# Stage ends and norms handled by token tile in a twelve-block transformer on one core

## The reference

```
x = x + cross_attention(layernorm(x), context of 4096 tokens, masks)   # 16 heads of 16
x = x + mixing(layernorm(x))
x = x + feed_forward(layernorm(x))
```

## Time and profile before

| | us |
|---|---|
| median of 3 runs | 1506.76 |
| the three runs | 1506.76, 1503.57, 1507.40 |
| span of the profiled execution (first to last instruction) | 1502.7 |
| time of the profiled execution, apart from its span | not given |
| median less span | 4.06 |
| busy: PE, DVE, ACT, POOL | 1371.0, 1010.4, 857.6, 567.3 |
| mean granted clock of TensorE, as a share of 2.4 GHz | 0.965 |

### The profile page before, as it was taken

How to read it: one execution, slowest core, us unless ns; L and a number is a source line. 1 busy time by engine, 2 the same in 40 slices (tenths; PEclk the granted TensorE clock), 3 DMA queues, 4 the chain that set the end, 5 groups by cost and what they waited for, 6 DMA issues and landing times. The chain is left out here.

```text
span 1502.7 us, 28955 instructions
## 1 busy us (share of the span) xinstructions
PE 1371.0 (91%) x10502; PEld 810.9 (54%) x10576; DVE 1010.4 (67%) x2314; ACT 857.6 (57%) x1308; POOL 567.3 (38%) x686
## 2 busy tenths in 40 slices
PE   8999797999999888699999888699999896999987
PEld 3766655455555456255555555255555582555555
DVE  4445486999999724778787053588884236888832
ACT  5143141899999621288888551167777211777762
POOL 4564252689989800655555340111110001111100
PEclk9999999799999978799999999899999998999999
DMA  8878998255456062266655195247776801667800
GB/s 265 280 255 256 245 258 274 33 77 83 65 82 146 2 89 39 53 96 90 88 81 143 59 185 202 75 71 109 104 113 190 118 9 45 96 96 108 156 2 8
DMA packets 126008, 178.30 MB, mean 119 GB/s; under 512 B 14733, under 2 KB 106021, under 8 KB 116646
## 3 DMA queue, kind: packets, MB, share of 16 engines
q1 hardware_dynamic: 111898, 161.04, 52.1%
q10 hardware_dynamic: 13968, 15.41, 3.4%
HBM read 132.58 MB, written 43.78 MB: 117 GB/s over the span
## 5 line engine op out<-in xcount | busy, mean ns | idle before, releaser
L1003 ACT ACTIVATE prob_a<-ps 128x1024 f32<-128x1024 f32 x464 | 456.6, 1020 | 142.7 <-PE ps L835 95.4
L818 PE MATMUL ps<-kop,qop 116*128 116x512 bf16 x1024 | 344.9, 401 | 37.4 <-DMA qop<-qparts 22.9
L1027 DVE TENSOR_REDUCE best_a<-ps 128x1 f32<-128x512 f32 (+1 forms) x488 | 318.5, 709 | 48.9 <-PE ps L818 48.4
L835 PE MATMUL ps<-qop,kop 116*128 116x256 bf16 x2048 | 333.9, 274 | 7.1 <-ACT prob_a L1003 2.6
L835 PEld LDWEIGHTS ps<-qop,kop 116*128 116x128 bf16 x2048 | 193.8, 98 | 123.2 <-ACT prob_a L1003 20.7
L1023 DVE CUSTOM_DVE_ANT_0 dump_a<-ps,neg_q 128x512 bf16<-128x512 f32 (+1 forms) x244 | 165.7, 715 | 43.5 <-PE ps L818 41.3
L862 PE MATMUL ps<-prob_a,vop_a 128*32 128x256 f32 x3072 | 191.7, 383 | 3.1 <-POOL prob_a L1167 2.2
L818 PEld LDWEIGHTS ps<-kop,qop 116*128 116x128 bf16 x1024 | 95.3, 103 | 162.4 <-issue 65.5
L1137 POOL TENSOR_TENSOR used_a<-prob_a,gT 128x1024 f32<-128x1024 f32 x64 | 153.2, 2396 | 23.6 <-DVE used_a L1040 17.0
L1116 POOL CAST mpart_a<-nmax_a 128x2 bf16<-128x2 f32 x64 | 26.4, 412 | 351.9 <-DVE nmax_a L1032 351.9
L1167 POOL TENSOR_TENSOR prob_a<-prob_a,neg_k 128x1024 f32<-128x1024 f32 x48 | 102.5, 2135 | 92.0 <-ACT prob_a L1001 86.4
(11 more groups left out here) (337 smaller groups left out, 1823.1 us busy)
## 6 DMA issues: line engine op xcount, KB each, us to landing
kop<-kparts SPq DMA_DIRECT2D x448, 128.0 KB, 5.1
kparts<-kp SPq DMA_DIRECT2D x64, 384.0 KB, 4.5
vals<-vst SPq DMA_DIRECT2D x16, 1024.0 KB, 5.3
vraw<-vals SPq DMA_DIRECT2D x64, 256.0 KB, 6.6
e_w<-in_e_w SPq DMA_DIRECT2D x4, 2048.0 KB, 11.0
z_w<-in_z_w SPq DMA_DIRECT2D x24, 256.0 KB, 6.8
ctxT<-in_ctxT SPq DMA_DIRECT2D x8, 512.0 KB, 8.1
raw<-in_mask ACTq DMA_DIRECT2D x16, 256.0 KB, 5.5
```

What stands on the lines that cost most here:

```text
L818: return pe.matmul(out, qop[0:R_ALL, h, t * P:(t + 1) * P], kop[0:R_ALL, h % UNROLL, j * CHUNK:(j + 1) * CHUNK], start=True, stop=True)
L835: ins = pe.matmul(st_bank(n)[:, j * NT:(j + 1) * NT], kop[0:R_ALL, h % UNROLL, k * P:(k + 1) * P], qop[0:R_ALL, h, :], start=(j % 2 == 0), ...
L1003: act.activation(prob[:, n % NP, :], st_bank(n), ACT.Exp).then_inc(S("exp_done"), 1)
L1027: dve.tensor_reduce(out, bank, AX.X, ALU.max).then_inc(sem, 1)
```

## The change

Six things are done. Statistics of x (bn_stats) are taken at the end of the old block, tile by tile, right behind the addition of the tile; the new block starts with bn_aggr. The output matmuls of a tile go to a bank of their own with a signal of their own, and DVE adds one tile at a time (stream_out_pe, add_stream_dve). turn_pe waits for, transposes and signals each tile by itself, into banks 0 and 3, and ACT copies each tile by itself (two copies of 256 columns for one of 512; in frames and the recurrence four of 128 for two of 256). NORM_FILL goes from 16 to 8. In the queries of layer 1, 14 mask matmuls stay ahead of the norm and 18 go behind the projection. POOL's clearing in attend (layers 1 to 3), taylor and frames waits until both tiles are normalised. The places not shown repeat those shown, block by block; the scores' and probabilities' transpositions elsewhere stay as they were.

```diff
-NORM_FILL, FOLD_FILL, TOP_FILL = 16, 6, 28
+NORM_FILL, FOLD_FILL, TOP_FILL = 8, 6, 28
+MASKS_FIRST = 14
...
-def norm_dve(c, dve, S, src, dst, n=0):
-
-    for t in range(QT):
-        dve.bn_stats(c.stats[:, t, :], src[:, t, :]).then_inc(S("norm_stats"), 1)
-    dve.wait_ge(S("norm_stats"), QT * (n + 1))
+def measure_dve(c, dve, S, t):
+
+    dve.bn_stats(c.stats[:, t, :], c.x[:, t, :]).then_inc(S("x_measured"), 1)
+
+
+def moments_dve(c, dve, S):
+
     for t in range(QT):
         dve.bn_aggr(c.moments[:, t, :], c.stats[:, t, :]).then_inc(S("norm_moments"), 1)
-    dve.wait_ge(S("norm_moments"), QT * (n + 1))
+    dve.wait_ge(S("norm_moments"), QT)
+
+
+def norm_dve(c, dve, S, src, dst):
+
+    moments_dve(c, dve, S)
     dve.tensor_scalar(c.var[:, :], c.moments[:, :, 1], EPS, None, ALU.add).then_inc(S("norm_var"), 1)
-    dve.wait_ge(S("norm_rstd"), n + 1)
+    dve.wait_ge(S("norm_rstd"), 1)
     for t in range(QT):
         dve.tensor_scalar(dst[:, t, :], src[:, t, :], c.moments[:, t, 0:1], c.rstd[:, t:t + 1],
                           ALU.subtract, ALU.mult).then_inc(S("norm_done"), 1)
 
-def norm_pool(c, pool, S, n=0):
-
-    pool.wait_ge(S("norm_var"), n + 1)
+def norm_pool(c, pool, S):
+
+    pool.wait_ge(S("norm_var"), 1)
     pool.tensor_tensor(c.rstd[:, :], c.var[:, :], c.minus_half[:, :], ALU.pow).then_inc(S("norm_rstd"), 1)
 
-def turn_pe(c, pe, S, src, bank, name):
-
-    for ct in range(CT):
-        for t in range(QT):
-            ins = pe.transpose(c.ps[:, bank, ct * NT + t * P:ct * NT + (t + 1) * P],
-                               src[:, t, ct * P:(ct + 1) * P], c.ident[:, :])
-    ins.then_inc(S(name), 1)
+TURN_BANKS = (0, 3)
+
+
+def turn_pe(c, pe, S, src, name, done=None):
+
+    for t in range(QT):
+        if done is not None:
+            pe.wait_ge(S(done), t + 1)
+        for ct in range(CT):
+            ins = pe.transpose(c.ps[:, TURN_BANKS[t], ct * P:(ct + 1) * P], src[:, t, ct * P:(ct + 1) * P], c.ident[:, :])
+        ins.then_inc(S(name), 1)
+
+
+def turned(c, t):
+
+    return c.ps[:, TURN_BANKS[t], 0:D].rearrange("p (m n) -> p m n", m=CT)
 
...
-def add_stream_dve(c, dve, S, bank):
-
-    dve.tensor_tensor(c.x[:, :, :], c.ps[:, bank, :].rearrange("p (t d) -> p t d", t=QT), c.x[:, :, :],
-                      ALU.add).then_inc(S("x_added"), 1)
-    dve.wait_ge(S("x_added"), 1)
+def stream_out_pe(c, pe, S, banks, srcT, w, n_ct=CT, ready=None, n=0):
+
+    for t in range(QT):
+        if ready is not None:
+            pe.wait_ge(S(ready), QT * n + t + 1)
+        for ct in range(n_ct):
+            ins = pe.matmul(c.ps[:, banks[t], 0:D], srcT[:, ct, t * P:(t + 1) * P], w[:, ct, :],
+                            start=(ct == 0), stop=(ct == n_ct - 1))
+        ins.then_inc(S("out_psum"), 1)
+
+
+def add_stream_dve(c, dve, S, banks, measured=True):
+
+    for t in range(QT):
+        dve.wait_ge(S("out_psum"), t + 1)
+        dve.tensor_tensor(c.x[:, t, :], c.ps[:, banks[t], 0:D], c.x[:, t, :], ALU.add).then_inc(S("x_added"), 1)
+        dve.wait_ge(S("x_added"), t + 1)
+        if measured:
+            measure_dve(c, dve, S, t)
+    if measured:
+        dve.wait_ge(S("x_measured"), QT)
...
+    def sum_masks(pe, first, end):
+
+        for k in range(first, end):
+            ins = pe.matmul(c.ps[:, 7, 0:NT], c.idle[:, 0:P], c.neg_k[:, k, :], start=(k == 0), stop=(k == KT - 1))
+        return ins
+
     @stage.tensor
     def _(pe):
         if l == SHIELDED:
-            for k in range(KT):
-                ins = pe.matmul(c.ps[:, 7, 0:NT], c.idle[:, 0:P], c.neg_k[:, k, :], start=(k == 0), stop=(k == KT - 1))
-            ins.then_inc(S("masks_summed"), 1)
+            sum_masks(pe, 0, MASKS_FIRST)
         else:
             keep_warm(c, pe, NORM_FILL)
-        pe.wait_ge(S("norm_done"), QT)
-        turn_pe(c, pe, S, c.xn, 0, "x_turned")
-        pe.wait_ge(S("xT_ready"), 1)
+        turn_pe(c, pe, S, c.xn, "turned", "norm_done")
+        pe.wait_ge(S("xT_ready"), QT)
         q.project(pe, S, banks)
+        if l == SHIELDED:
+            sum_masks(pe, MASKS_FIRST, KT).then_inc(S("masks_summed"), 1)
 
     @stage.scalar
     def _(act):
         act.activation(warm[:, :], c.ones[:, 0:1], ACT.Exp).then_inc(S("table"), 1)
-        act.wait_ge(S("x_turned"), 1)
-        act.activation(c.xT[:, :, :], c.ps[:, 0, :].rearrange("p (t n) -> p t n", t=CT), ACT.Copy)\
-           .then_inc(S("xT_ready"), 1)
+        turn_act(c, act, S)
         q.first_and_second(act, S, banks)
...
+        if asked is not None:
+            pool.wait_ge(asked.S("norm_done"), QT)
         pool.memset(mpart[:, :, :, :], 0.0).then_inc(S("cleared"), 1)
         pool.memset(vop[:, :, :, HD:32], 0.0).then_inc(S("cleared"), 1)
         pool.wait_ge(S("cleared"), 2)
...
         split(0)
         fill(1)
         pool.wait_ge(S("bias"), 16)
-        if asked is not None:
-            pool.wait_ge(asked.S("norm_done"), QT)
         pool.tensor_tensor(c.x[:, :, :], c.x[:, :, :], c.bo[:, :].unsqueeze(1).to_broadcast((P, QT, D)), ALU.add)\
...
         pe.wait_ge(attended.S("s_read"), attended.reads)
-        turn_pe(c, pe, S, c.att, 0, "att_turned")
-        pe.wait_ge(S("attT_ready"), 1)
+        turn_pe(c, pe, S, c.att, "turned")
         pe.wait_ge(attended.S("wo"), 16)
-        by_tokens_pe(c, pe, [c.ps[:, 1, t * D:(t + 1) * D] for t in range(QT)], c.xT, c.wo[:, :, :],
-                     None).then_inc(S("out_psum"), 1)
+        stream_out_pe(c, pe, S, (1, 4), c.xT, c.wo, CT, "xT_ready")
 
     @stage.scalar
     def _(act):
-        act.wait_ge(S("att_turned"), 1)
-        act.activation(c.xT[:, :, :], c.ps[:, 0, :].rearrange("p (t n) -> p t n", t=CT), ACT.Copy)\
-           .then_inc(S("attT_ready"), 1)
+        turn_act(c, act, S)
 
     @stage.vector
     def _(dve):
-        dve.wait_ge(S("out_psum"), 1)
         dve.wait_ge(attended.S("bias_added"), 1)
-        add_stream_dve(c, dve, S, 1)
+        add_stream_dve(c, dve, S, (1, 4))
 
     return stage
 
-def turn_act(c, act, S, bank=0, n=0):
-
-    act.wait_ge(S("turned"), n + 1)
-    act.activation(c.xT[:, :, :], c.ps[:, bank, :].rearrange("p (t n) -> p t n", t=CT), ACT.Copy)\
-       .then_inc(S("xT_ready"), 1)
+def turn_act(c, act, S, n=0):
+
+    for t in range(QT):
+        act.wait_ge(S("turned"), QT * n + t + 1)
+        act.activation(c.xT[:, :, t * P:(t + 1) * P], turned(c, t), ACT.Copy).then_inc(S("xT_ready"), 1)
 
...
             norm_pool(c, pool, S)
+            pool.wait_ge(S("norm_done"), QT)
             pool.memset(vop[:, :, :, HD:32], 0.0).then_inc(S("vop_zero"), 1)
             pool.wait_ge(S("vop_zero"), 1)
             pool.memset(vop[:, :, :, HD:HD + 1], 1.0).then_inc(S("vop_ones"), 1)
...
         @block.tensor
         def _(pe):
             keep_warm(c, pe, NORM_FILL)
-            pe.wait_ge(S("norm_done"), QT)
-            turn_pe(c, pe, S, c.xn, 0, "turned")
-            pe.wait_ge(S("xT_ready"), 1)
+            turn_pe(c, pe, S, c.xn, "turned", "norm_done")
+            pe.wait_ge(S("xT_ready"), QT)
             for name in ("q", "k", "v", "o"):
                 pe.wait_ge(weights.S(name), 16)
             for w, bank, name in ((wq, 1, "q_psum"), (wk, 3, "k_psum")):
...
-            dve.wait_ge(S("added"), QT * E)
+            for t in range(QT):
+                dve.wait_ge(S("added"), QT * (E - 1) + t + 1)
+                measure_dve(c, dve, S, t)
...
-def turn_scaled_act(c, act, S, scales, gb, bank=0):
-
-    act.wait_ge(S("turned"), 1)
+def turn_scaled_act(c, act, S, scales, gb):
+
     act.wait_ge(scales, 16)
-    for ct in range(CT):
-        act.activation(c.xT[:, ct, :], c.ps[:, bank, ct * NT:(ct + 1) * NT], ACT.Identity, scale=gb[:, 0, ct:ct + 1],
-                       bias=gb[:, 1, ct:ct + 1]).then_inc(S("xT_ready"), 1)
+    for t in range(QT):
+        act.wait_ge(S("turned"), t + 1)
+        for ct in range(CT):
+            act.activation(c.xT[:, ct, t * P:(t + 1) * P], turned(c, t)[:, ct, :], ACT.Identity,
+                           scale=gb[:, 0, ct:ct + 1], bias=gb[:, 1, ct:ct + 1]).then_inc(S("xT_ready"), 1)
 
...
             for t in range(QT):
                 for g in range(G):
-                    ins = pe.matmul(c.ps[:, 3, t * D:(t + 1) * D], spread[:, g, t, :], result[:, g, :],
+                    ins = pe.matmul(c.ps[:, 2 + t, 0:D], spread[:, g, t, :], result[:, g, :],
                                     start=(g == 0), stop=(g == G - 1))
-            ins.then_inc(S("out_psum"), 1)
+                ins.then_inc(S("out_psum"), 1)
...
-            turn_pe(c, pe, S, hT, 3, "h_turned")
+            for t in range(QT):
+                for m in range(CT):
+                    ins = pe.transpose(c.ps[:, 2 + t, m * P:(m + 1) * P], hT[:, m, t * P:(t + 1) * P], c.ident[:, :])
+                ins.then_inc(S("out_psum"), 1)
...
-            by_tokens_pe(c, pe, halves(c, 7), hT, w2, None, HT).then_inc(S("out_psum"), 1)
+            stream_out_pe(c, pe, S, (7, 1), hT, w2, HT)
...
```

(1 more changed line is left out.)

104 lines of the change are left out of this document (45 added, 59 removed).

## The result

| | before | after |
|---|---|---|
| median of the runs shown, us | 1507.08 (4 runs, 1503.57 to 1509.35) | 1490.57 (4 runs, 1488.90 to 1494.87) |
| ratio to before, 95% interval | | 0.9896 [0.9867, 0.9925] |
| span of the profiled execution, us | 1502.7 | 1487.5 (the run itself: 1488.9) |
| granted clock, mean | 0.965 | 0.963 |

The change is faster by 16.5 us between these medians, about 1%. Forecast were 1489.0 and a range of 1484 to 1497. By the two ratios the change is worth 16 and 13 us, and their intervals together reach from 8 to 20. Left out of all medians and ratios here are two executions in a slow state, one of e3 (4433 us) and one of the kernel before beside e1 to e4 (1540 us).

A forecast was written before the change was run, and what follows sets the result against it. Serial work at stage borders, one engine at a time, was taken as the bound. Gains 2.2 + 4.9 + 0.2 + 5.8 + 4.2 + 0.9 = 18.2 us took the span from 1502.7 to 1484.5; plus 4.1, rounded up: 1489.0, range 1484 to 1497.

The forecast's parts named there:

- Norm to projection: Six stages, normalised tiles to projection, by tile with half the fillers: 1.92 becomes 0.96, gain 5.8 us in all.
- Add and statistics by tile: Eight stage ends, last psum to aggregation: 2.04 becomes 1.43, gain 0.61 each, 4.9 us in all.
- from transposition to aggregation: Sign in the changed profile: first transposition of att to the aggregation takes 4.3 us where there were 5.3.
- rival D: Gain taken back downstream, layers' starts waiting for something not moved: half the sum lost, 1498 us; chance 0.06.
- Queries: Queries of layers 1 to 3: normalisation gains 0.97 and the way to the projection 0.44 each, 4.2 us together.
- The moved mask matmuls: Layer 1's queries: 18 of 32 mask matmuls go behind the projection; POOL has 1.01 us to spare, cost 0.
- Scaled copies: Frames and recurrence: four copies of 128 columns for two of 256; gains 0.6 and 0.3, 0.9 us in all.
- the prediction's own signs: Failure signs: qop memset over 2 us or late, clock at 0.50 in the projections, or longer stages between borders.
- Rival A: Queries: POOL holds VectorE's qop memset, as the two exclude one another; + 4.5, 1493.5 us; chance 0.14.
- Rival B: TensorE's clock falls at a few borders, 1.7 us lost at each; four cost 6.8, 1495.8 us; chance 0.12.
- Rivals C and E: C: clock falls at all ten filler borders, 1523 us, 0.03. E: tiles wait for one another, some 1503, 0.03.
- The split rule: VectorE's fixed cost per instruction: with nothing overlapped, the 8 split adds and 5 copies would cost about 2 us.

The follow-up runs named there:

- e3: Changed kernel with GpSimd's clearing no longer waiting for the norm: 1495.38 us, ratio 0.9920 to the kernel before.
- e1: Changed kernel with 16 fillers at the norm again instead of 8: 1507.89 us, ratio 1.0013 to the kernel before.
- e4: Changed kernel with both statistics of x back behind the block boundary, additions still split: 1493.38 us, ratio 0.9905 to the kernel before.
- e9: Changed kernel with the norm's transpositions and copy whole again, not by tile: 1497.91 us, ratio 0.9947 to the kernel before.
- e5: Kernel before with 8 fillers instead of 16, nothing else: 1508.04 us, ratio 1.0025 to the kernel before.
- e10: Changed kernel with stage ends whole again (one turn and copy, one PSUM tile, one addition): 1511.57 us, ratio 1.0040 to the kernel before.
- e11: Changed kernel measured again on another chip, no edit: 1493.76 us, ratio 0.9912 to the kernel before.
- e7: Changed kernel with short fillers (masks at layer 1's queries) in TensorE's idle gaps at the borders: 1486.72 us, ratio 0.9869 to the kernel before.
- e6: Kernel before with GpSimd's clearing waiting for the norm, nothing else: 1501.12 us, ratio 0.9981 to the kernel before.
- e2: Changed kernel with no fillers at the norm instead of 8: 1511.39 us, ratio 1.0031 to the kernel before.
- e8: Changed kernel with 24 more fillers behind the queries' projection of layers 1 to 3: 1489.64 us, ratio 0.9893 to the kernel before.
- e12: Changed kernel with the edits of e7 and e8 together: 1487.94 us, ratio 0.9873 to the kernel before.

## Why the prediction was right

**The terms of the chain** hold at the borders where the clock stayed up. Norm to projection was forecast as 1.92 to 0.96, and measured 0.96 there; e9 isolates one part of it (0.48 by the split) and e5 the other (0.52 by the fillers). Add and statistics by tile was 2.04 to 1.43 and measured 1.45; from transposition to aggregation 4.3 was forecast and 4.37 measured, and e10 puts this part of the change at 7.7 by its chain, where 2.2 and 4.9 were forecast. Where nothing fell, the intervals moved as forecast: plain 1.54 for 1.57, zone 1.08 for 0.96, frames 1.12 for 1.21, and in e11 the feed forward 1.18 for 1.23. Two didn't, the choosing experts (0.63 for 1.57, see rival D) and Taylor (2.69 for 2.01), whose stages hold low clock before and after.

**Queries.** 0.97 and 0.44 were forecast for each; layers 2 and 3 gained 1.40 and 1.39 at the projection. In layer 1 the low clock left 0.71, and of it only 0.09 arrived at the first score (13.82 for 13.91 behind the aggregation). In e7, whose projection there was at 2.96, it was 13.01, so 0.90 of 1.39 arrived. The moved mask matmuls aren't the reason: they end at 599.64, the first scores wait for the load of qop until 605.54, and POOL's six operations leave 1.15 to spare before the first row maxima (616.22 above) where they left 1.01 before. So their cost is 0, as forecast. Layer 2, where no mask was moved, passed on 0.58 of its 1.40 to the first score, layer 3 all of it; how much arrives there varies with the load of qop.

**Scaled copies.** Taken as 0.37 for one of 128 columns, four in about 1.5, and 1.67 from the tile to the projection. Measured were 0.46 for one, 1.51 for four and 1.83 to the projection: the gain was 0.52 for frames and 0.14 for the recurrence, 0.7 in sum instead of 0.9.

**The sum and its luck.** The sum was too large. The 4.1 us around the span were the distance of a median to the span of another, quicker run; a run is 1.2 to 1.5 longer than its own span. So the forecast amounts to the median before less 18.2, and measured were 16.5 between the medians, 13 by e11's ratio, and 15.2 between the profiled spans. Of those 15.2, the 3.4 ahead of the first changed border came by chance, so the borders gave 11.8 where 18.2 was forecast. That 1490.57 lies so near to 1489.0 is in part luck; 1493.76 lies in the range as well. By the prediction's own signs, the chain, the pairs of xn and the memset came as said, but the clock did read 0.50 in three projections, and two stretches, those of the recurrence and the feed forward, became longer. What the sum left out is the clock: the stretches from the queries of layer 1, the recurrence and the feed forward became longer by 1.7 together where a gain of 3.9 was forecast, and the wait for weights in the choosing experts.

**Rival A** fell with its premise. I had read from DVE's memset starting 0.48 behind the norm, just when POOL's copy ended, that the two exclude one another. In the changed kernel the memset starts 0.49 behind the norm and runs from 594.20 for 1.76, beside POOL's memset of 594.14 and its copy of 595.42, as long as in the earlier trace rows, where POOL was idle beside it; e6 shows the same. The coincidence was a gap of issue, which the row even names so. The normalisation, on the other hand, is held: 1.70 with POOL's memset beside it (e3), 0.73 without. Of the Trainium skill's rule (GPSIMD Engine Reference, 1. Specifications, contention with VectorE at the shared interface) the traces bear out the case of the normalisation; VectorE's memset isn't held. I had also counted q's subtraction among the instructions with two SBUF inputs; of its inputs one is ps, which is PSUM.

**Rival B** was there, at two or three borders of an execution of the changed kernel (three in the first, in e11 the queries of layers 1 and 3), and its price was about right: 1.7 lost at the recurrence, 1.5 at the feed forward, 0.7 at the queries' projection. The recurrence, for which I had counted TensorE busy 1.5 in the stretch, was among them with 1.72; the plain border, counted as 2.1, had 1.95 and no fall behind it. What I had missed is the other side of the account. The change also shortens TensorE's waits for copies, from 0.69 to 0.35 ahead of the out projection and from 0.69 to 0.47 ahead of the norm's, and the mean clock over the runs, 0.962 to 0.963 before and after, shows no net loss. That these shorter waits are what balances the missing fillers is argued, not shown. Shown are the parts: with whole ends (e10) or with no fillers (e2) many borders fall, and with the gaps bridged (e7) those of the profiled execution don't. The Trainium skill (TensorE: Matmul & The Clock Gate, on oscillation) asks for short idle gaps, and by it I had expected no fall, since no gap was to be over 2 us. The traces differ: in the stretch ahead of a fall the longest gap was 1.33 at the recurrence and 1.03 in e5 (zone experts, 1196.6 to 1200.0), and 2.12 in e10.

**Rival D** came true at one stage, with a small part of its price. I had named the weights of the choosing experts, and I had read from the kernel before that TensorE doesn't wait for weights. Now it does at this place, 0.83 us in the changed kernel and 2.26 in e11, and 0.8 to 1.5 in e3, e4, e7, e8 and e12. In e1, e2, e9 and e10, where TensorE comes to that half later, it waits less than 0.3 for them. The other stages passed on what they got (plain, zone, e9). Issuing that load earlier wasn't tried.

**Rivals C and E** fell: the clock fell at no more than three borders in a profiled execution of the changed kernel, and the first tile was handled beside the second at every border.

**The split rule.** In the prediction the Trainium skill's advice of 512 elements or more (VectorE: DVE Perf Modes, TRN2 errata) was weighed against the cover by other work. The runs decide: at an end the split costs VectorE 0.14 in additions (0.42 and 0.41 for 0.69), as forecast, and 0.10 in statistics (two of 0.43 for 0.76), and it gains 0.66 there, 0.49 ahead of the out projection and 0.48 at the norm.

**My expectations of the experiments** held for the chain nearly everywhere, and for the times only in e4. Some misses are no larger than the 3 us between two measurements of one kernel (e3, e9, e11 and e12 came 1 to 3 us above their ranges, e7 0.3 below). Six say more. For e1 I had sized the hold at 1.4 and hoped for a better clock; it is 1.6, and the clock doesn't rise: 6 us short. For e2 and e5 the falls cost more than I had allowed, by 3 and 1. For e8 I had counted on 3 to 7 us that didn't come. For e6 I had 1 us, and 3.8 were measured. For e10 I had the chain and not the clock, and was 14 us short, 10 of them against e11.

## What to carry to other kernels

Split a hand-over by tile only where the first tile's step runs beside the second's, and then cut down what was there to fill the old gap: without that second step (e1) the whole gain of 16 us was gone, and without the first (e5) the second was a loss. Price each gap of TensorE at a border twice, by the chain and by what the granted clock does behind it; e10 lost about as much by the second as by the first, or more. See which loads are issued inside the stage: they don't move with the norm, and a faster norm can run into them (the choosing experts). And before a filler is added somewhere, see whether anything urgent runs in the time that it keeps warm (e7 against e8).

## What the runs showed of the chip beyond that

Averaged over the kernel, a microsecond of TensorE at the low level goes with 0.2 to 0.4 us of time: from e2, 20.8 us for 64; within the executions of one kernel on one chip (nine sets of 10 to 24) 0.6 to 1.2 us for each 0.001 of mean clock, which is 3 us at the low level; and in the part ahead of the first changed border, nearly the same in all fourteen profiles, 0.35 (it ends at 528.39 with 20.5 us of low clock and at 534.96 with 38.5). Where TensorE itself is the chain it is half, as at the recurrence (1.7 for 3.4), and in e8 16 us less of it gave nothing that the times can tell. And executions of one kernel differ by up to 13 us (1498.47 to 1511.87 for the kernel before beside e5 to e8; 1486.48 to 1497.39 in e11): at which borders the clock falls differs from one to the next, and a single profile can't tell a change of 4 us in the whole time from chance. Only the stretches in which the clock stayed up can.
